# Moving the W3 product of a row tile from the third quarter of a period into the second quarter of the next

## The reference, cut to what matters

```
x = x + tanh(g_xattn) * mamba(ctx, z=layernorm(x))      # selective scan over 512 steps, 512 channels, 16 states
h = silu(Q(layernorm(x)) @ W1.T) * (Q(layernorm(x)) @ W2.T)   # Q: rms norm, gains, rounding to 8 bits per row
x = x + tanh(g_ffn) * (Q(h) @ W3.T)                      # W1, W2, W3 rounded to -1, 0, 1 times a scale
```

## Time and profile before

| | us |
|---|---|
| median of 3 runs | 814.97 (814.53 to 815.8) |
| the profiled execution | 812.6 |
| its span in the trace | 810.8 |
| busy: PE, DVE, ACT, POOL | 620.2, 673.3, 550.5, 548.2 |

### The profile page before, as it was taken

One profiled execution on the slowest core, in us unless ns is written; L12 is line 12 of the kernel. 1 busy time (PEld: TensorE's weight loads), 2 busy tenths in 40 slices (PEclk: granted clock), 3 DMA queues, 4 the chain that ended last, 5 costly groups with the idle time before them and its releaser, 6 DMA issues.

```text
span 810.8 us, 7802 instructions
## 1 busy us (share of the span) xinstructions
PE 620.2 (76%) x2260; PEld 239.7 (30%) x2260; DVE 673.3 (83%) x808; ACT 550.5 (68%) x797; POOL 548.2 (68%) x288
## 2 busy tenths in 40 slices
PE   6555557786679696979787878987887969686985
PEld 3211112434252232323232222232322323233442
DVE  3489887787787989899989999898989898957663
ACT  4587954744969586776767685959595867556671
POOL 2027376948487878778777797787878687865631
PEclk9766677796869596877778685959595959697997
DMA  4488852627931111143111111134111020000000
GB/s 99 98 279 270 322 149 65 205 67 187 285 89 31 50 39 46 46 95 87 50 49 37 45 46 26 57 91 104 39 50 42 27 52 27 13 14 0 27 14 26
DMA packets 38457, 67.80 MB, mean 84 GB/s; under 512 B 10848, under 2 KB 13408, under 8 KB 36240
## 3 DMA queue, kind: packets, MB, share of 16 engines
q1 hardware_dynamic: 38416, 67.31, 29.1%
HBM read 46.32 MB, written 4.46 MB: 63 GB/s over the span
## 4 chain that ended last, share of the span: by engine, by line
PE 38%; DVE 28%; ACT 11%; issue 10%; POOL 10%; DMA 2%; SPq 1%; DVEq 0%; ACTq 0%; POOLq 0%
PE ring L1432 11%; DVE hb L1019 11%; PE y_ps L1410 7%; PE ring L1497 7%; PE du_ps L1397 5%; DVE dbu_ps L1010 5%; POOL hb L589 3%; POOL h L567 3%; ACT dA L765 3%; PE ring L1345 2%; DVE u L965 2%; ACT L907 2%; POOL hb L567 2%; DVE h_max L1166 2%; PE ring L1369 1%
## 5 line engine op out<-in xcount | busy, mean ns | idle before, releaser
L589 POOL TENSOR_TENSOR hb<-hb,bc_rep 128x2048 f32<-128x2048 f32 x63 | 284.9, 4522 | 101.9 <-DVE hb L1019 91.5
L1019 DVE TENSOR_TENSOR_SCAN hb<-dA,dbu_ps 128x1024 f32<-128x1024 f32 x128 | 292.2, 2283 | 16.7 <-ACT dA L765 9.5
L1010 DVE TENSOR_TENSOR dbu_ps<-du_ps,bc_rep 128x1024 f32<-128x1024 f32 x128 | 157.7, 1232 | 31.8 <-PE du_ps L1397 26.7
L765 ACT ACTIVATE dA<-dl_rep,a_neg 128x511 f32<-128x511 f32 x252 | 160.7, 710 | 14.8 <-DMA dl_rep<-delta 9.7
L1397 PE MATMUL du_ps<-du,sel_q 32*128 32x512 f32 x128 | 100.3, 874 | 54.1 <-DVE dbu_ps L1010 54.1
L1410 PE MATMUL y_ps<-hb,sel_s 128*32 128x512 f32 x512 | 124.2, 630 | 1.5 <-POOL hb L589 1.5
L1497 PE MATMUL ring<-w3T,hT 128*128 128x512 fp8e4 x256 | 92.3, 530 | 20.0 <-issue 20.0
L574 POOL TENSOR_TENSOR h<-h,up_sb 128x1024 f32<-128x1024 f32 x24 | 56.5, 2355 | 19.0 <-ACT up_sb L783 18.8
L567 POOL TENSOR_TENSOR h<-h,g3b 128x1024 f32<-128x1024 f32 x24 | 56.1, 2358 | 14.3 <-ACT work L843 13.9
L1345 PE MATMUL ring<-ident,yz 128*128 128x128 f32 x64 | 15.5, 387 | 54.0 <-DVE yz L1137 54.0
L544 POOL TENSOR_TENSOR delta<-delta,relu 128x512 f32<-128x512 f32 x15 | 19.0, 1267 | 54.9 <-DVE delta L989 54.9
(11 more groups left out here) (167 smaller groups left out, 998.8 us busy)
## 6 DMA issues: line engine op xcount, KB each, us to landing
dl_rep<-delta SPq DMA_DIRECT2D x252, 64.0 KB, 2.0
bc_rep<-bc_scratch SPq DMA_DIRECT2D x32, 256.0 KB, 5.0
h<-in_L_ffn_w_dram SPq DMA_DIRECT2D x8, 1024.0 KB, 7.5
x<-in_L_ffn_w_dram SPq DMA_DIRECT2D x8, 1024.0 KB, 6.4
up_sb<-in_L_ffn_w_dram SPq DMA_DIRECT2D x8, 1024.0 KB, 6.3
xt<-in_x_dram SPq DMA_DIRECT2D x16, 256.0 KB, 3.4
out_dram<-x SPq DMA_DIRECT2D x16, 256.0 KB, 2.0
ctx_nat<-in_ctx_dram SPq DMA_DIRECT2D x4, 512.0 KB, 5.3
```

Of the source, the lines that this page charges most:

```text
L589: g.tensor_tensor(hb[:, s % 4, :, :], hb[:, s % 4, :, :], c_rep(s // 16), ALU.mult)\
L765: ins = a.activation(dA[:, s % 2, i, 1:L], dl[:, 1:L], ACT.Exp, scale=a_neg[:, s % 16, i:i + 1])
L1010: v.tensor_tensor(dbu_ps[:, :, :], du_ps[:, :].unsqueeze(1).to_broadcast([P, 2, L]), b_rep(b)[:, 2 * half:2 * half + 2, :], ALU.mult).then ...
L1019: v.tensor_tensor_scan(hb[:, s % 4, 2 * half:2 * half + 2, :].rearrange("p a l -> p (a l)"), dA[:, s % 2, 2 * half:2 * half + 2, :].rearra ...
```

## The change

PE's `down` of a row tile moves from quarter q = 2 of period g + 5 to quarter q = 1 of period g + 6, behind `dt_proj(k + 1)` and ahead of `transpose_yz(k - 1)`. DVE's `output` moves from q = 3 of period g + 5 to q = 1 of period g + 6, behind `gated_y`. SP's store goes with it, from q = 3 to q = 1, and the reload of x, which stood a quarter later than the store, now stands directly behind it. Where et = 1, `add_scan(k - 1)` moves from q = 1 to q = 2, since it may need the reloaded rows. The last `down` of the loop, row tile 10, now stands after it. `LAG_O` is 6. The number of instructions stays the same.

```diff
             if q == 1:
                 if k + 1 < KQ:
                     jobs.append(("dt", k + 1))
+                if k >= LAG_O:
+                    jobs.append(("down", k - LAG_O))
                 if k >= 1:
                     jobs.append(("yzT", k - 1))
             if q == 2 and g >= 0:
-                jobs += [("hT", g, 0), ("hT", g, 1), ("down", g)]
+                jobs += [("hT", g, 0), ("hT", g, 1)]
...
-    jobs += [("yzT", KQ - 1), ("aT", TAIL)]
+    jobs += [("down", KQ - LAG_O), ("yzT", KQ - 1), ("aT", TAIL)]
...
-                    if q == 0 and k >= LAG_O and k + 2 < NT:
-                        reload_x1(k + 2)
-                    if q == 3 and k >= LAG_G:
-                        store_out(k - LAG_G)
...
+                    if q == 1 and k >= LAG_O:
+                        store_out(k - LAG_O)
+                        if k + 2 < NT:
+                            reload_x1(k + 2)
                     if s == TERN_AT + WCH:
                         load_x1(1)
-            for ft in range(KQ - LAG_G, NT):
+            for ft in range(KQ - LAG_O, NT):
                 store_out(ft)
...
-                    if q == 3 and g >= 0:
-                        output(g)
...
                     if q == 1 and k >= 1:
                         gated_y(k - 1)
+                    if q == 1 and k >= LAG_O:
+                        output(k - LAG_O)
+                    if q == 2 and et == 1:
+                        add_scan(k - 1)
                     if q == 2:
                         z_bias(k)
                         if f >= 0:
...
                         st = mark(v.bn_aggr(zmv[:, :], zst[:, :]))
-                        if k >= 1:
+                        if k >= 1 and et != 1:
                             add_scan(k - 1)
                         after(st)
                         z_var(k)
...
             last_times_c()
+            output(KQ - LAG_O)
             gated_y(KQ - 1)
             add_scan(KQ - 1)
...
-            def down(ft, s_next=None):
+            def down(ft):
 
...
                 for t in range(H // P):
-                    if t == 4 and s_next is not None:
-                        bcast_du(s_next)
                     ins = mm(dst[:, :], hT[:, t, :], w3T[:, t, :], start=(t == 0), stop=(t == H // P - 1))
                 ins.then_inc(done, 1)
 
...
                     if q == 1:
                         if k + 1 < KQ:
                             dt_proj(k + 1)
+                        if k >= LAG_O:
+                            down(k - LAG_O)
                         if k >= 1:
                             transpose_yz(k - 1)
                         bcast_du(s + 1)
...
                     if q == 2:
                         if g >= 0:
                             transpose_hidden(g)
-                            down(g, s + 1)
-                        else:
-                            bcast_du(s + 1)
+                        bcast_du(s + 1)
...
+            down(KQ - LAG_O)
             sum_states(2 * KQ - 1)
             transpose_yz(KQ - 1)
```

## The result

The changed kernel takes 811.75 us (median of 10 runs, 810.01 to 814.24), against 814.75 for the kernel before in 10 runs beside it. The ratio is 0.9965, with a 95% interval of 0.995 to 0.9979. The profiled execution took 810.8 with a span of 808.7; before, 812.6 and 810.8. The forecast was 812.0.

A forecast was written before the change was run, and what follows sets the result against it. DVE nearly bounds the periods, with PE's work between T and E making it wait. Terms -16.5 + 6.6 + 4.3 + 2.2 = -3.4, taken as -3, gave 812.0 us against 814.97; range 806 to 817.5.

The forecast's parts named there:

- E after T: From q = 2's first `add_input` (T) to the start of the 28 W1/W2 matmuls (E): 18.46 us falls to 16.8.
- T to the waiting scan: From q = 2's first `add_input` to next q = 1's scan: 1.65 us less per period, 16.5 in ten.
- the two waits at `output`: DVE's `output` in q = 1 waits for W3 in k = 7 and 11: 2.5 and 1.8 us, +4.3.
- scan to the next T: Additions in q = 1: `output` on DVE +6.6 us over ten periods, its two waits for W3 +4.3.
- last T to the end: After the loop W3 costs 3.5 us in full, E's gain there is only about 1.3: +2.2 us.
- signs of being wrong: `sum_states` in q = 3 over 6 us, `output` waiting every period, or an unlisted wait in DVE's dense stretch.
- nothing, within 0.5 either way: `add_scan` moved to q = 2 where et = 1: 0.7 us less ahead of T, 0.7 more behind, net nothing.
- SP's store and reload, the ring: Store and reload waiting for `output` in q = 1, and the ring's changed bank order: both cost nothing.
- B: Rival: nothing measurable, gains and additions cancel within 0.2%, 813.3 to 816.6 us; chance 0.25.
- A: Rival: E moves less, `sum_states` in q = 3 being slow; slower than 816.6, about 831 if cold throughout; chance 0.17.
- C: Rival: `output`'s waits in k = 7 and 11 absent or short, E low: 807.3, down to 805 us; chance 0.14.
- D: Rival: PE's clock stays up from q = 3 on, E at its floor every period: -13.1, 802 us; chance 0.04.

The follow-up runs named there:

- tail_w3: Changed kernel with row tile 10's W3 behind the last `yz` transposes and its `output` behind the tail's second row statistics: 809.05 us (0.9929).
- fill8_q2: Changed kernel with 8 unused matmuls behind q = 2's hidden transposes and 8 behind the following `bcast_du`: 806.44 us (0.9897).
- before_fill: Kernel before with 4 unused matmuls in q = 2 between the hidden transposes and W3: 797.65 us (0.979).
- before_w3x1: Kernel before with 1 of 16 W3 matmuls for row tiles 0 to 10, `bcast_du` following the one: 796.88 us (0.9782).
- fill_q2: Changed kernel with 8 unused matmuls behind q = 2's hidden transposes and 2 behind the following `bcast_du`: 811.34 us (0.9959).
- after_w3x1: Changed kernel with 1 of 16 W3 matmuls for row tiles 0 to 10: 802.7 us (0.9857).

## Why the prediction was right

| step | forecast | measured |
|---|---|---|
| E after T, mean | 16.8 | 16.90 |
| T to the waiting scan, ten periods | -16.5 | -13.3 |
| the two waits at `output` | 2.5, 1.8 | 2.53, 1.79 |
| scan to the next T, ten periods | +10.9 | +9.0 |
| last T to the end | +2.2 | +2.25 |
| DVE's wait for `du_ps`, for `exps` | 2, 8 | 1.9, 3.7 |

**W3 leaves, the row tile is next, the clock rises late.** As told. `sum_states` began 9.4 to 9.5 after T in six periods (9.55 forecast), 10.9 in k = 6, and 10.2 to 10.3 in k = 5, 9 and 13. It took 5.08 us in the mean (5.12, by the early run of the earlier trace rows). The rise fell between T + 11.4 and T + 14.5, against my 11.1 to 14.3, and E moved by 1.49 in the mean, not 1.65. In k = 8 the rise was latest and `sum_states` took 6.10 us. Over 6 us was one of my signs of being wrong; it came in one period of ten. Another sign, a wait of DVE that is on none of my lists, came too: `fsc`, 1.4 us in all.

**The gain in the periods was mis-sized by 3.2 us of 16.5.** 1.6 of it is E itself (18.39 to 16.90 by the same measure, -14.9 in ten periods). The rest is the floor of DVE. I had put DVE's own way to the waiting scan at T + 25.6 and held E to decide in every period. In six periods DVE came there without a wait: at T + 25.9 to 26.0 in k = 7, 11 and 12, and at T + 27.0 to 27.1 in k = 5, 9 and 13; 474.07 above, with no bracket, is T + 27.13. So E decided in only four of the ten, and DVE's wait for `exps` is 3.7 instead of 8.

**`add_scan` was put at nothing, and costs.** k = 5, 9 and 13 are the periods with et = 1, where it now stands behind T. DVE's way to the scan is 1.1 us longer there than in k = 7, 11 and 12: 0.7 for `add_scan`, 0.4 to 0.5 for the new wait for `fsc`. `add_scan` also stands ahead of the row tile's `quant_scales`, so `sum_states` begins 0.8 later. Ahead of T it gives back only 0.5, as the next paragraph shows, so my "nothing, within 0.5 either way" was too low. No run has the change without this shift.

**What the change put in.** The two waits are exact, since each was the difference of two rows. `output` in q = 1 cost less than its 6.6: the rest of +9.0 is 4.7 us. Two things make up the 1.9. From the scan of k = 8 and of k = 12 to the next T, where `add_scan` has left, the change adds 0.16 and 0.13 us instead of 0.66, which is 1.0 less in the two together. In k = 11, 13 and 14 it adds 0.32, 0.26 and 0.36, since DVE now comes later to inputs of POOL that it waited for: the 0.92 us ahead of the second `h_max` shrink to 0.59 in k = 11 and to 0.53 in k = 13, and 0.34 ahead of `h_sc` in k = 14 are gone. That is another 1.0 less. (In k = 6 and 10 the rest is 0.15 over the forecast.)

```profile
565.11 1.22 DVE L1168 TENSOR_REDUCE h_max<-h 128x1 f32<-128x1024 f32 x1 [0.59 <-POOL h L569]
```

Both misses, 3.2 too much gained and 1.9 too much given back, partly cancel, and so the total came out closer than its terms: that part of the agreement is luck.

**The end.** +2.25 against 2.2. DVE's two waits there are the 7.36 for W3 and the 2.82 for `y_ps` above, together 10.2, where one wait near 10 was forecast. `tail_w3` took 3.3 back by putting W3 out of that path.

**SP's store and reload, the ring.** No new wait on them is in the list of 255 to 690 us, so they cost nothing that the profile shows.

**The rivals.** B, nothing measurable, was missed by a hair: the interval ends at 0.9979, and B began at 0.998. A was near: the mean E, 16.90, lies 0.25 below the point where the change would have paid nothing. C did not come, the waits were there. D did not either: at the `du_ps` product ahead of the row tile's transposes the clock was down in all ten periods (2.04 us each). The prediction had said the same of the kernel before from two windows; it holds there in all ten as well. (In its (2), W3 at 1.2 GHz would end at 486.8, not 486.5; nothing rests on it, as W3 ran at 1.00.) `fill8_q2` brought E near D's floor in most periods (16.17 in the mean, against 15.9), and gained 5 us where D had 10 below the forecast. There too DVE's own way is the longer one. The rule of the Trainium skill ("TensorE: Matmul & The Clock Gate", section "HAM oscillation — how this bites in real kernels"), to close the pauses between the engine's work, speaks for what `before_fill` does. The trace agrees in k = 9, where the clock was at 1.00 ahead of `du_ps`; in four periods the next pause undid it.

**What the prediction did not see.** It called W3 a cost of the path in q = 2. That is true while the clock is down there, as `before_w3x1` shows. With 4 unused matmuls the kernel before loses its wait for `du_ps` with W3 in place, and leaving W3 out on top of that gains nothing. So W3's length and the low clock are one cost that can be removed by either end: the path's reading holds for how the move got at it, and the clock's says that the move was not needed for it. The move won back about what the low clock had cost, and paid for most of it in new places. My own expectation of `before_fill`, 806 to 811, failed for the same reason. I had not counted that `bcast_du`, the transposes and the end come out quicker as well.

## What to carry to other kernels

Before moving work off a path, look at the granted clock where the path starts: if it is down, and the engine is not the one that bounds the kernel, try a few unused matmuls in the pause ahead of it first, and look in every period whether the next pause undoes them. When a step moves to another place in a dense engine's order, subtract two rows for every place where its input is late (here it gave 2.5 and 1.8 to the tenth), and take the dense engine's own way through the period as a floor from a period in which it doesn't wait. A gain that is forecast from one engine ends where that floor begins.

## What the runs showed of the hardware

The clock can rise and fall again within a few microseconds. In `fill_q2` it was 1.00 from 457 to 460 us, PE stood idle for 1.5 us up to 460.14, and it was at 0.50 from 461 to 462; in `before_fill` PE was also idle for 0.75 us at 1.00 in k = 9, and it stayed up, but after 1.32 us in k = 12 it was down. Four unused matmuls, 1.9 us of PE at the low clock, were worth 17 us of 815 over a kernel with eleven such periods. And the start-up, ahead of the first of these periods, took different times in the profiles: T of k = 5 was at 273.26 in the changed kernel's profile and at 277.38 in that of `after_w3x1`, whose instructions up to there are the same. Whether one kernel varies by as much is not shown, since each was profiled once. A difference of a few microseconds between two single profiles is therefore read by period, not by span.
